# Attention steps of a macaron block: the value products moved behind the transposes and the scores

## The reference

```python
q = hidden_states @ w_q.T                      # 16 heads of 32
kv = hidden_states @ w_kv.T                    # one k and one v head of 32, shared by all heads
attn = jnp.einsum('bnih,bjh->bnij', q, k)
attn = jnp.where(causal, -jnp.finfo(attn.dtype).max, attn)
attn = jax.nn.softmax(attn, axis=-1)
out = jnp.einsum('bnij,bjd->bind', attn, v)
out = out.reshape(B, S, N_HEADS * HEAD_DIM) @ w_proj.T + b_proj
...
x = x + 0.5 * ffn(layernorm(x))
x = x + attention(layernorm(x))
x = x + 0.5 * ffn(layernorm(x))
```

## Time and profile before

| | |
|---|---|
| median of 3 runs | 2860.82 us (2860.53 to 2860.98) |
| profiled execution, its own time | 2862.31 us |
| its span, first to last instruction | 2860.5 us |
| PE busy | 2758.7 us, 96% of the span, 15648 matmuls |
| VectorE, ScalarE, GpSimd busy | 65%, 40%, 11% |
| mean granted clock of TensorE | 0.985 |
| attention, steps K = 1 to 127 | from 1154.3 us to about 1752 us of the span |

### The profile page before, as it was taken

The page is one execution under the profiler, slowest core; times in us unless marked ns, Lnnn a source line. Parts: engine busy times, 40 slices in busy tenths (PEclk is TensorE's granted clock), DMA queues, the critical chain, the costliest instruction groups (busy, mean ns, idle before and its releaser), DMA issues. The chain is left out here.

```text
span 2860.5 us, 42018 instructions
## 1 busy us (share of the span) xinstructions
PE 2758.7 (96%) x15648; PEld 2210.2 (77%) x15648; DVE 1848.7 (65%) x3487; ACT 1139.9 (40%) x2432; POOL 317.4 (11%) x347
## 2 busy tenths in 40 slices
PE   7999999999999996899999997999999999999998
PEld 5888888888888884667667665788888888888887
DVE  5667656766676665666666665656766676676655
ACT  3333333333333321776776774333323333333331
POOL 0000000000000002354554420000000000000000
PEclk9999999999999997899999998999999999999999
DMA  3211311121121103000000002211121122202100
GB/s 122 98 46 32 116 45 44 60 89 44 48 78 64 47 1 112 1 9 31 27 27 31 16 16 104 103 45 44 59 89 44 48 79 78 66 26 103 45 15 30
DMA packets 65022, 156.12 MB, mean 55 GB/s; under 512 B 6864, under 2 KB 6992, under 8 KB 64592
## 3 DMA queue, kind: packets, MB, share of 16 engines
q1 hardware_dynamic: 64848, 153.77, 15.9%
HBM read 128.58 MB, written 25.17 MB: 54 GB/s over the span
## 5 line engine op out<-in xcount | busy, mean ns | idle before, releaser
L350 PE MATMUL bank<-xnt_h,wgu_h 128*128 128x512 f32 x2048 | 803.3, 392 | 10.2 <-issue 7.4
L350 PE MATMUL bank<-xnt_h,wgu_l 128*128 128x512 f32 x2048 | 799.1, 390 | 0.0
L350 PE MATMUL bank<-xnt_l,wgu_h 128*128 128x512 f32 x2048 | 798.6, 390 | 0.0
L507 DVE TENSOR_TENSOR h<-bank,sg 128x512 f32<-128x512 f32 x256 | 176.9, 691 | 600.5 <-PE bank L350 586.7
L350 PEld LDWEIGHTS bank<-xnt_h,wgu_h 128*128 128x128 f32 x2048 | 385.7, 188 | 90.6 <-issue 8.6
L350 PEld LDWEIGHTS bank<-xnt_h,wgu_l 128*128 128x128 f32 x2048 | 385.4, 188 | 81.1
L350 PEld LDWEIGHTS bank<-xnt_l,wgu_h 128*128 128x128 f32 x2048 | 385.7, 188 | 79.1
L446 ACT ACTIVATE mag<-h 128x512 f32<-128x512 f32 x256 | 162.0, 633 | 702.2 <-DVE h L507 702.2
L369 PE MATMUL bank<-wd_h,hs_h 128*128 128x512 f32 x1024 | 400.3, 391 | 9.1 <-DVE hs_l L542 9.1
L369 PE MATMUL bank<-wd_l,hs_h 128*128 128x512 f32 x1024 | 399.7, 390 | 0.0
L369 PE MATMUL bank<-wd_h,hs_l 128*128 128x512 f32 x1024 | 399.6, 390 | 0.0
(11 more groups left out here) (114 smaller groups left out, 3276.4 us busy)
## 6 DMA issues: line engine op xcount, KB each, us to landing
raw_gu<-in_w_gu SPq DMA_DIRECT2D x128, 512.0 KB, 4.8
raw_d<-in_w_d SPq DMA_DIRECT2D x128, 256.0 KB, 2.6
x_mid<-x_sb SPq DMA_DIRECT2D x64, 256.0 KB, 2.0
x_sb<-in_x SPq DMA_DIRECT2D x32, 256.0 KB, 4.8
x_sb<-x_mid SPq DMA_DIRECT2D x8, 1024.0 KB, 6.1
x_sb<-x_mid SPq DMA_DIRECT2D x32, 256.0 KB, 4.8
out<-x_sb SPq DMA_DIRECT2D x32, 256.0 KB, 2.1
probs<-in_w_q SPq DMA_DIRECT2D x1, 1024.0 KB, 5.8
```

Source lines behind the costliest of these rows:

```text
L350: last = pe.matmul(ps, w[:, r, kind, k], xs[:, b, k], start=(i == 0), stop=(i == 3 * KD - 1))
L507: v.tensor_tensor(h[:, r], bank[UP + r % 2][:, :], sg[:, r % 2], ALU.mult).then_inc(h_done, 1)
```

## The change

In `step` of PE, `weigh(K - 1)` moves from behind the projection to the end of the step, and `turn_q` moves from the end of the step to before the scores. All transposes of a step then stand in one run with the projection, and scores and value products follow.

```diff
                         if i >= 1:
                             turn_probs(K, 1)
                         project(B, k)
-                        if K > 0:
-                            weigh(K - 1)
                         for j in range(2, i + 1):
                             turn_probs(K, j)
                         if k % TT == TT - 1:
...
                             if k == TURN_K:
                                 turn_k(nxt)
+                            if k in TURN_Q:
+                                turn_q(nxt, TURN_Q[k])
                         if K + AHEAD < ALL:
                             scores(K + AHEAD)
-                        if nxt < BATCHES:
-                            if k in TURN_Q:
-                                turn_q(nxt, TURN_Q[k])
+                        if K > 0:
+                            weigh(K - 1)
```

## The result

The changed kernel takes 2877.03 us, median of six runs (2873.45 to 2877.72), beside 2860.68 for the kernel before: a ratio of 1.0056 [1.0045, 1.0067], 16 us slower. 2873 was predicted, with a range of 2860 to 2883. The profiled execution took 2877.61 us, its span is 2875.8.

The account below looks back on a forecast made before the run. PE was taken as the bound, busy 76.1 of 78.2 us a batch. Batches 1 to 5 +5.8, batch 0 +2.4, batch 6 +0.6, batch 7 +2.2, clock +1: +12 on 2860.8, so 2873 us, range 2860 to 2883.

Parts of the forecast that it names:

- Passages: PE switching kinds of work: 83 runs fewer at 0.15 us, 12.5 us less; scores to value products taken as 0.85 and 1.07.
- Steps 2 and 6: Attention steps 2 and 6 of batches 1 to 5: -0.15 us each.
- Steps 7 and 8: Scores wait for VectorE's masks, value products now come behind: 4.22 and 3.49 us, +0.35 a pair; 3 and 4 likewise.
- Step 9: `scale_output` starts late and holds the masks behind it: PE stalls 1.5 us, step 6.04 against 4.56, +1.5.
- Step 5: Late `scale_output` without statistics behind it: scores at 3.93 us into the step, +0.15.
- Step 11: q turned earlier ends the wait for the sums' drain, 0.4 us new bank wait: 5.35 against 6.45, -1.1.
- Steps 14 and 15: Chain through GpSimd's split of x keeps the scores in place, 12 value products now follow: +0.8 in six batches.
- Steps 10, 12, 13: One pair of passages between kinds of PE work fewer in each: -0.2 us each, -0.6 together.
- the last batch: Batch 7, no projection at k = 1 and 5 (+0.9 each): +2.2 in all, plus +1 for a lower clock.
- only passages count: Rival: mask waits and late `scale_output` stay hidden, 83 runs fewer give 12.5 us: 2848; chance 0.10.
- gains and waits cancel: Rival: step 9's stall is half, steps 14/15 keep 0.5 us, whole at +3: 2861 to 2866; chance 0.20.
- the clock falls in every batch: Rival: step 9's stall lowers PE's clock in batches 1 to 5, +1.7 us each: 2881 to 2890; chance 0.12.

Follow-up runs that it names:

- e3: The changed kernel with the value products ahead of the scores again in steps k = 0, 4, 8 and 12; 2851.97 us, ratio 0.9968.
- e8: The changed kernel with VectorE's `scale_output` issued behind the next step's masks at k = 5 and 9 only; 2860.55 us, ratio 1.0004.
- e2: The changed kernel with q's transposes back behind scores and value products, so `weigh` alone is moved; 2884.37 us, ratio 1.0087.
- e5: The changed kernel with GpSimd splitting x before it widens the sums at k = 14; 2867.50 us, ratio 1.0025.
- e6: The changed kernel with the edits of e3 and e5 joined; 2842.57 us, ratio 0.9939.
- e7: The kernel before with q's transposes ahead of the scores and e5's edit of GpSimd's queue, `weigh` not moved; 2850.27 us, ratio 0.9964.
- e4: The changed kernel with VectorE's `scale_output` issued behind the next step's masks at k = 1, 5 and 9; 2868.53 us, ratio 1.0033.
- e9: The changed kernel with `weigh` in its old place in batch 7 alone; 2869.73 us, ratio 1.0036.

## Why the prediction was right, step by step

**Slower by waits, not by work**: right. The forecast of each batch 1 to 5 was +1.15, measured +1.1 (+1.3 in the third): +5.8 over the five, for 5.8. Batch 6 gave +0.6 for 0.6. Batch 0 gave +2.4 for 2.4, but this sum is met partly by luck: step 9 lost 1.9 where 1.3 was forecast, and step 10 gained 1.0 (5.67 to 4.69) where 0.2 was.

**Passages.** Right. Steps 2 and 6 gave 0.14 for 0.15. The passage from scores to value products, which no row of before showed, is like its nearest row: 1343.05 to 1343.90 and 1346.15 to 1347.22 are 0.85 and 1.07 us, the numbers taken.

**Steps 7 and 8**: 4.21 and 3.53 for 4.22 and 3.49; the bracket in step 8 is 0.80 for "about 0.8". **Step 9**: 5.91 in four batches and 6.14 in the third, for 6.04; the bracket there is 1.49 for 1.5, and e3 and e8 show, by undoing one side each, that it is `scale_output` waiting ahead of the masks. **Step 5**: +0.22 for +0.15. **Step 11**: 5.40 for 5.35 (the terms that the prediction writes for it add up to 5.28), and the drain's wait is gone, which e2 confirms by bringing it back; from the transposes of x to those of q it takes 0.73 us (1362.68 to 1363.41), 0.3 more than a block's 0.44, at the place where I put 0.4. That this is the wait for a bank is not shown. **Steps 14 and 15**: +0.76 together (10.83 to 11.59) for +0.8, and e5 shows the cause. **Steps 10, 12, 13**: -0.20, -0.18 and -0.19 for -0.2 each.

**The term that was mis-sized is the last batch**, as the prediction put it: "pairs, k = 1 and 5, less at its end: +2.2" and "One more such stretch of 3 us costs 1.5; I take +1". Measured are +5.2 for 3.2. The stalls and the clock are not what was wrong. The scores of step 1 came 4.01 us into it (1702.70 to 1706.71), for 3.93, and e8, which had the same stall of 2.92 us in step 1 at the full clock, took 4.80 us for that step beside 3.85 before, for the 0.9 forecast. A low stretch adds 1.3 or 1.4 us to such a pair of steps (steps 1 and 2 of after 5.19 and 4.39, 5 and 6 5.34 and 4.39; with the full clock in e8 4.80 and 3.51), and there were two instead of one.

What the prediction left out are steps 2 and 6 of this batch, to which it gave only the saved passages. PE in step 2 before, and in step 6 of e8, both at the full clock:

```profile
1696.36 1.09 PE L954 MATMUL bank<-ident,probs 128*128 128x128 f32 x8
...
1698.66 0.71 PE L945 MATMUL bank<-kt,qt 32*128 32x256 f32 x8
```

```profile
1711.62 1.53 PE L954 MATMUL bank<-ident,probs 128*128 128x128 f32 x12
1713.91 0.71 PE L945 MATMUL bank<-kt,qt 32*128 32x256 f32 x8 [0.77 <-DVE nmax L1199]
```

The scores stand 2.30 and 2.29 us into the step in both orders, where VectorE's masks put them once no projection covers these; only the value products that filled the time before now come behind. The step is 3.51 us for 2.94: +0.57 each, where -0.15 was forecast, 1.4 us in all. With 0.3 for the clock and 0.3 for small ones that is the missing 2.0. It is the mechanism of step 8, at a place where the prediction did not look for it.

The remaining 1.4 us of the profiled difference lie ahead of the first instruction that the change moves. The starts of that step in the eleven traces lie between 1153.6 and 1155.7, though all these kernels are the same up to there, so this is scatter between executions and not a term.

**The rivals.** That only passages count (2848) is out: they are worth something, since e6 has a batch 1.4 us shorter than e7, but they are not all that the change does. That gains and waits cancel is out by the ratio's interval. That the clock falls in every batch is out: after stalls of 1.49 us it is 1.00 in the windows above.

**Two expectations missed.** e3 came out at 2852 for 2856 to 2860. The steps that it names came within 0.1 us of it; not priced were step 13 of the first batch, 1.1 us shorter, and the steps in batches 6 and 7 whose value products complete a head group, and 2.6 us lie outside the attention steps. e4 came out at 2868.5 for 2861 to 2863: I had not asked which queue, GpSimd's, starts later when a VectorE instruction does; e8 settled it. e2 (2884.4 for 2882) and e9 (2869.7 for 2872) are off by no more than those parts of the program differ that the edits do not reach.

## What to carry to other kernels

Two things decide what a move of work costs: what is queued behind the instruction that waits for it, and which wait it used to fill. Find, for each moved group, its last consumer, see what stands behind that one in its own queue, and ask whether PE still has a filler long enough for it. Ask it again for the stretches where other filler is missing, here the last batch. Fewer passages between kinds of work are worth their price only where no wait ends the step: here savings estimated at 12.5 us ended in a kernel 16 us slower, and with one group in four put back and the order of two tasks of GpSimd exchanged, nearly the same order was 17 us faster than before.

## What the runs showed of the hardware

**VectorE beside GpSimd.** The same `TENSOR_TENSOR` of 128x64 from SBUF takes 214 ns in the median of e8 and 1297 in e4, where GpSimd adds 128x512 tiles beside it, six times as long; the one of 128x128 takes 279 ns at its shortest and 898 in the median of e8, beside the end of GpSimd's additions, and 1217 in e4's. The Trainium skill (Perfetto Trace Analysis, Optimizing Scalar/DVE Operations) says that GpSimd and DVE share an SBUF read port. The rows agree with a shared resource, and they show who pays: the four additions took 5.05 us in e4 and 5.03 before, where nothing of the rotation ran beside them. In e4's trace they end at 1314.12, 1315.40 and 1316.63 (the last three), and the three rows of the rotation end 0.15, 0.09 and 0.09 us behind them: each VectorE instruction came through only with the end of an addition. The masks, which read a bank and one tile, kept their 0.29 us beside the same additions (1312.84 in e4).

**PE's clock.** Stalls of PE of 1.25 to 1.49 us in steady work left the clock at 1.00; after 2.57 us in the kernel before and 2.92 us in the changed one it was 0.50, the 1.2 GHz level, for over 3 us. After one of 1.97 us it was 1.00 in step 1 of e9's last batch (1703.72 to 1707.00) and 0.50 in step 5 (above), and likewise in the kernel before. After one of 2.32 us in e6 it was 0.50 in step 1 of the last batch (1676.22) and 1.00 in step 5 (1691.80). So the length of the stall alone does not decide it.
